# The up product of an sLSTM feed-forward as three half-precision products, features split by GpSimd, convolution sums in a row

## The reference, cut to what matters

```python
xn = ln(x);  xc = silu(causal_conv(xn, 4 taps))
wx = [gi(xc), gf(xc), gz(xn), go(xn)]            # 64x64 matrices per head
raw = wx_t + h @ rk + b                          # per token, in order
lfm = m + log_sigmoid(fr);  mn = max(ir, lfm)
cn = exp(lfm-mn)*c + exp(ir-mn)*tanh(zr);  nn = exp(lfm-mn)*n + exp(ir-mn)
h  = sigmoid(og) * cn / nn
x  = x + groupnorm(h)
x  = x + (gelu(g) * v) @ wd,  [g, v] = ln(x) @ wu     # 256 -> 2 x 336 -> 256
```

## Time and profile before

| | us |
|---|---|
| median of 3 runs | 4049.7 (4048.94 to 4052.33) |
| profiled execution | 4048.4 |
| its span, first to last instruction | 4046.7 |

### The profile page before, as it was taken

How to read it: one execution, slowest core, us unless ns; L and a number is a source line. 1 busy time by engine, 2 the same in 40 slices (tenths; PEclk the granted TensorE clock), 3 DMA queues, 4 the chain that set the end, 5 groups by cost and what they waited for, 6 DMA issues and landing times. The chain is left out here.

```text
span 4046.7 us, 170045 instructions
## 1 busy us (share of the span) xinstructions
PE 3876.7 (96%) x70778; PEld 2189.0 (54%) x70778; DVE 3681.0 (91%) x10771; ACT 3256.1 (80%) x6720; POOL 2211.6 (55%) x2425
## 2 busy tenths in 40 slices
PE   6999999999999999999999998799999999999997
PEld 3555555555555555555555554466666666666664
DVE  7999999999999999999999998788888888888886
ACT  4999999999999999999999998466666666666665
POOL 3666666666666666666666666444344443444443
PEclk9999999999999999999999999899999999999998
DMA  2000111000000000000000000000000001000000
GB/s 77 21 23 23 48 54 51 21 23 23 21 23 23 21 23 23 21 23 23 21 23 23 21 23 24 17 22 23 31 24 23 23 22 33 23 22 22 26 21 9
DMA packets 101034, 105.27 MB, mean 26 GB/s; under 512 B 17536, under 2 KB 96032, under 8 KB 99768
## 3 DMA queue, kind: packets, MB, share of 16 engines
q1 hardware_dynamic: 100264, 94.39, 8.0%
HBM read 48.68 MB, written 17.69 MB: 16 GB/s over the span
## 5 line engine op out<-in xcount | busy, mean ns | idle before, releaser
L596 POOL TENSOR_TENSOR conv_products<-normed_features,conv_taps_by_token 128x256 f32<-128x256 f32 (+1 forms) x852 | 780.4, 916 | 609.7 <-DVE convolved_features L549 358.5
L309 PE MATMUL banks<-up_centred,after_cell_features 128*32 128x336 f32 x9088 | 759.6, 452 | 0.0
L786 POOL TENSOR_TENSOR exps_of_both_halves<-scores 128x256 f32<-128x256 f32 x512 | 419.1, 842 | 619.9 <-ACT scores L1042 614.7
L285 PE MATMUL banks<-down,hidden_features 112*32 112x256 f32 x6816 | 427.5, 384 | 0.0
L365 ACT ACT_TABLE_LOAD x284 | 364.4, 1283 | 52.7 <-PE banks L265 47.8
L586 POOL TENSOR_TENSOR conv_partial_sums<-conv_products,conv_partial_sums 128x512 f32<-128x512 f32 x284 | 364.8, 1285 | 66.6 <-DVEq L485 44.4
L1042 ACT ACTIVATE scores<-scores 128x512 f32<-128x512 f32 x512 | 305.4, 626 | 116.3 <-DVE scores L1190 115.4
L309 PEld LDWEIGHTS banks<-up_centred,after_cell_features 128*32 128x32 f32 x9088 | 237.2, 109 | 270.6 <-issue 270.6
L386 ACT ACT_TABLE_LOAD x284 | 364.4, 1283 | 5.0
L1190 DVE SCALAR_TENSOR_TENSOR scores<-banks,score_top 128x512 f32<-128x512 f32 x512 | 327.7, 681 | 27.0 <-PE banks L872 26.4
L258 PE MATMUL banks<-recurrent_weights,h_features 64*32 64x256 f32 x9088 | 311.7, 383 | 1.4 <-ACT h_features L358 1.4
(11 more groups left out here) (215 smaller groups left out, 10055.6 us busy)
## 6 DMA issues: line engine op xcount, KB each, us to landing
layer_inputs<-layer_outputs SPq DMA_DIRECT2D x284, 96.0 KB, 2.0
layer_inputs<-in_x SPq DMA_DIRECT2D x285, 32.0 KB, 1.8
x_scratch<-layer_outputs SPq DMA_DIRECT2D x284, 32.0 KB, 1.8
x_tokens<-in_x SPq DMA_DIRECT2D x32, 256.0 KB, 3.1
context_features<-in_ctx SPq DMA_DIRECT2D x32, 256.0 KB, 3.8
layers_out<-x_scratch SPq DMA_DIRECT2D x32, 256.0 KB, 2.9
out<-result SPq DMA_DIRECT2D x64, 128.0 KB, 1.8
up_centred<-in_ff_up SPq DMA_DIRECT2D x1, 2688.0 KB
```

The lines of the kernel that those rows point to most:

```text
L285: mm = nc.tensor.matmul(bank[group(l), FD, 0:D], hidt[:, i, group(l)], down[:, l, i, :], start=i == 0, stop=i == UTILES - 1, skip_group_ch ...
L309: mm = nc.tensor.matmul(bank[group(l), b, 0:UP], xmt[:, n, group(l)], up[:, l, n, at:at + UP], start=n == 0, stop=n == HALF - 1, skip_grou ...
L596: nc.gpsimd.tensor_tensor(prod[:, i:i + n], xnt[:, j % NRING].rearrange("p n t -> p (n t)")[:, None, :].broadcast_to([P, n, HALF * P]), ta ...
L786: nc.gpsimd.tensor_tensor(psum[:, i % RING, :], pr[:, i % RING, 0:S], pr[:, i % RING, S:2 * S], ALU.add).then_inc(halves_added, 1)
```

## The change

**Up product.** Its weights `up` are scaled by 16 and split, ahead of the first step, into two half-precision parts `up_hi` (ACT) and `up_lo` (DVE). In each step the features `xmt` are split by POOL into `xmt_hi` (a cast) and `xmt_lo` (a subtraction). The product is then hi x hi + lo x hi + hi x lo; the factor 1/16 goes into `rs2`, which POOL makes from the reciprocal standard deviation. PE waits for `xmt_hi` ahead of the up product and for `xmt_lo` ahead of its last part.

**POOL.** The sums of 256 columns no longer wait for DVE; they follow `rs2` in a row. The products no longer wait for DVE either; the first waits for the copy of xn, and the others follow the split.

**Around them.** `centred` multiplies both heads at once by a block with zeros (8 matmuls of 128 columns, not 16 of 64). h is one instruction of 256 columns on DVE and is transposed by four plain matmuls. DVE makes `yn` and `xm` earlier. ACT copies xn's features ahead of Gelu, and the hidden features at the start of the next step. `up`, `rows` and `rows_rest` lie in memory that the second stage fills later.

```diff
+            def feed_up_gate(j):
+                pe.wait_ge(xmt_hi_done, j + 1)
+                for part in range(2):
+                    for n in range(HALF):
+                        feed_up(UPG, 0, n, part, first=part == 0 and n == 0)
+                for part in range(2):
+                    feed_up(UPV, UP, 0, part, first=part == 0)
+                pe.wait_ge(xmt_split, j + 1)
+                for n in range(HALF):
+                    feed_up(UPG, 0, n, 2, last=n == HALF - 1)
+                feed_up(UPV, UP, 0, 2)
...
-            def feed_up(b, at, n):
+            def feed_up(b, at, n, part, first=False, last=False):
+                w_, x_ = ((up_hi, xmt_hi), (up_lo, xmt_hi), (up_hi, xmt_lo))[part]
...
-                        for odd in range(2):
-                            r = slice(DH * odd, DH * odd + DH)
-                            at = UP + n * DH
-                            mm = nc.tensor.matmul(bank[group(l), UPG + odd, at:at + DH], ht[r, n, group(l)], gnc[r, l, n, :],
-                                                  start=n == 0, stop=True, skip_group_check=True)
+                        mm = nc.tensor.matmul(bank[group(l), UPG + n, UP:UP + P], ht[:, n, group(l)],
+                                              gnc[:, l, n].rearrange("p r d -> p (r d)"), start=True, stop=True, skip_group_check=True)
...
-                transposes(FD, D, h, ht_ready)
+                for n in range(HALF):
+                    for odd in range(2):
+                        i = odd * HALF + n
+                        mm = nc.tensor.matmul(bank[DH * odd:DH * odd + DH, FD, D + n * P:D + (n + 1) * P], h[:, i * DH:(i + 1) * DH], ident[:],
+                                              start=True, stop=True, skip_group_check=True)
...
-                for n in range(HALF):
-                    nc.vector.scalar_tensor_tensor(out=h[:, n * P:(n + 1) * P].rearrange("p (r d) -> p r d", r=2), in0=heads_of(ot[:], n),
-                                                   scalar=1.0, in1=heads_of(half_r[:], n), op0=ALU.add,
-                                                   op1=ALU.mult).then_inc(h_done, 1)
+                nc.vector.scalar_tensor_tensor(out=h[:], in0=ot[:], scalar=1.0, in1=half_r[:], op0=ALU.add,
+                                               op1=ALU.mult).then_inc(h_done, 1)
...
-                pool.wait_ge(xn_done, j + 1)
+                pool.wait_ge(rstd_step, 2 * j + 2)
+                nc.gpsimd.tensor_scalar(rs2[:], rs[:, HEADS:HEADS + 1], 1.0 / UP_SCALE, None, ALU.mult).then_inc(rs2_done, 1)
                 nc.gpsimd.tensor_tensor(new[:, 2], prod[:, 2], old[:, 3], ALU.add).then_inc(conv_shifted, 1)
-                pool.wait_ge(d_ready, j + 1)
                 nc.gpsimd.tensor_tensor(new[:, 3], prod[:, 3], old[:, 4], ALU.add).then_inc(conv_shifted, 1)
-                pool.wait_ge(xnt_copied, j + 1)
                 pool.wait_ge(conv_done, j + 1)
                 pool.wait_ge(conv_shifted, 2 * j + 2)
-                for i, n, after, count in ((0, 1, xm_done, j + 1), (1, 1, cell_step, 3 * j + 1), (2, 2, xs_done, j + 1)):
-                    pool.wait_ge(after, count)
+                pool.wait_ge(xnt_copied, j + 1)
...
+                conv_taps(0, 1)
+                pool.wait_ge(xmt_copied, j + 1)
+                if j > 0:
+                    pool.wait_ge(up_done, j)
+                nc.gpsimd.tensor_copy(xmt_hi[:], xmt[:]).then_inc(xmt_hi_done, 1)
+                pool.wait_ge(xmt_hi_done, j + 1)
+                nc.gpsimd.tensor_tensor(xmt_lo[:], xmt[:], xmt_hi[:], ALU.subtract).then_inc(xmt_split, 1)
+                conv_taps(1, 1)
+                conv_taps(2, 2)
```

More of the change, by code:

```diff
@@ L120, in slstm @@
     BIAS = 2 * 512
-    rows = sb("bias_rows", [3 * LAYERS, BIAS])
-    rows_rest = sb("bias_rows_rest", [3 * LAYERS, BIAS])
+    lent = kept["sums"][:].rearrange("p a n -> p (a n)")
+    rows, rows_rest = lent[0:3 * LAYERS, 0:BIAS], lent[0:3 * LAYERS, BIAS:2 * BIAS]
+    pieces = kept["pieces"]
     rows_hi, rows_mid, rows_lo = (sb("bias_hi", [3 * LAYERS, BIAS], F16), sb("bias_mid", [3 * LAYERS, BIAS], F16),
@@ L305, in hidden_features @@
                 mm.then_inc(hidt_ready, 1)
-            def feed_up(b, at, n):
+            def feed_up(b, at, n, part, first=False, last=False):
+                w_, x_ = ((up_hi, xmt_hi), (up_lo, xmt_hi), (up_hi, xmt_lo))[part]
                 for l in range(LAYERS):
-                    mm = nc.tensor.matmul(bank[group(l), b, 0:UP], xmt[:, n, group(l)], up[:, l, n, at:at + UP], start=n == 0,
-                                          stop=n == HALF - 1, skip_group_check=True)
-                return mm
+                    mm = nc.tensor.matmul(bank[group(l), b, 0:UP], x_[:, n, group(l)], w_[:, l, n, at:at + UP], start=first, stop=last,
+                                          skip_group_check=True)
+                return mm
+            def feed_up_gate(j):
[9 more added lines that the diff above has]
+                feed_up(UPV, UP, 0, 2)
             def feed_up_last():
-                feed_up(UPV, UP, 1).then_inc(up_done, 1)
+                for part in range(3):
+                    mm = feed_up(UPV, UP, 1, part, last=part == 2)
+                mm.then_inc(up_done, 1)
             pe.wait_ge(w_step, UP_SCALED)
@@ L361, in both @@
                 return ap.rearrange("p n t -> p (n t)")
+            for l in range(LAYERS):
+                for m in range(HALF):
+                    act.wait_ge(up_centred, HALF * l + m + 1)
+                    nc.scalar.activation(up_hi[:, l, m, :], up[:, l, m, :], ACT.Copy, scale=UP_SCALE).then_inc(up_hi_done, 1)
             act.wait_ge(first_gates, 1)
@@ L374, in _ @@
                 nc.scalar.activation(bank[:, FD, D:], spb[:], ACT.Ln, bias=1.0).then_inc(sp_step, 1)
+                if j > 0:
+                    act.wait_ge(hidt_ready, j)
+                    copy(both(hidt[:]), bank[0:UT, CV, 0:UTILES * P], hidt_copied)
                 act.wait_ge(gn_mv, HEADS * (j + 1))
@@ L388, in _ @@
                     act.wait_ge(up_done, j)
-                act.wait_ge(yn_done, j + 1)
-                nc.scalar.activation(gl[:], bank[:, UPG, 0:UP], ACT.Gelu, scale=rs[:, HEADS:HEADS + 1]).then_inc(gelu_done, 1)
                 act.wait_ge(xnt_ready, j + 1)
                 copy(both(xnt[:, j % NRING]), bank[:, CV, 0:D], xnt_copied)
+                act.wait_ge(yn_done, j + 1)
+                act.wait_ge(rs2_done, j + 1)
+                nc.scalar.activation(gl[:], bank[:, UPG, 0:UP], ACT.Gelu, scale=rs2[:]).then_inc(gelu_done, 1)
                 act.wait_ge(decay_step, 2 * j + 2)
@@ L401, in _ @@
                 nc.scalar.activation(ct[:], part[:, j % 2, 0], ACT.Tanh).then_inc(ct_done, 1)
-                act.wait_ge(hidt_ready, j + 1)
-                copy(both(hidt[:]), bank[0:UT, CV, 0:UTILES * P], hidt_copied)
-            act.wait_ge(hidt_copied, STEPS)
+            act.wait_ge(hidt_ready, STEPS)
         @block.vector
@@ L412, in _ @@
                 nc.vector.memset(buf[:], val).then_inc(w_step, 1)
+                n += 1
+            for odd in range(2):
+                nc.vector.memset(gnc[DH * odd:DH * odd + DH, :, :, 1 - odd], 0.0).then_inc(w_step, 1)
                 n += 1
@@ L476, in _ @@
                     w_ = up[:, l, m, :].rearrange("p (k n) -> p k n", k=2)
[L477 to L478 removed]
+                    nc.vector.tensor_tensor(w_, w_, bank[:, 2 * l:2 * l + 2, 0:UP], ALU.subtract).then_inc(up_centred, 1)
+            for l in range(LAYERS):
+                for m in range(HALF):
+                    dve.wait_ge(up_hi_done, HALF * l + m + 1)
+                    nc.vector.scalar_tensor_tensor(out=up_lo[:, l, m, :], in0=up[:, l, m, :], scalar=UP_SCALE, in1=up_hi[:, l, m, :],
+                                                   op0=ALU.mult, op1=ALU.subtract).then_inc(up_split, 1)
+            dve.wait_ge(up_split, LAYERS * HALF)
             dve.wait_ge(w_step, n)
```

63 lines of the change are left out of this document (36 added, 27 removed).

## The result

The changed kernel takes 4418.4 us (median of 4 runs, 4408.1 to 4421.7), the kernel before beside it 4049.3 (4 runs). The ratio is 1.0906, with a 95% interval of 1.0886 to 1.0926: 369 us slower. The forecast was 4435, range 4090 to 4500. The profiled run took 4408.1 us.

A forecast was written before the change was run, and what follows sets the result against it. VectorE (DVE) was taken to set the step, with TensorE (PE) close behind. The profiled 4048 us plus 381 (284 steps x 1.34 us) plus 7 for set-up gave about 4435 us, range 4090 to 4500.

The forecast's parts named there:

- The turn: A DVE instruction reading two SBUF tensors waits until the POOL instruction under way is done, then needs 0.28 us.
- the timetable: One step laid out from Gelu's start, placing POOL's split and products against DVE; 1.34 us more a step, chance 0.45.
- The two dearest terms: DVE stalls behind POOL's products: convolved features behind the 512-column product, 1.10 us; h behind tap 1, 0.45 us.
- the hinge: h asks 0.15 us behind tap 1; slightly more POOL work ahead would give the milder turn, 4180 us, chance 0.30.
- the stall of after_cell: After-cell (xm) on DVE waits for POOL's second sum: 0.30 us a step.
- The step without stalls: DVE's step less the waits of lines 532 and 526 and h's second instruction: 8.16 us.
- The sum: Profiled 4048.4 us, plus 284 steps of 1.34 us, plus 7 us set-up: about 4435 us.
- DVE sets the step, with PE close behind.: In the kernel before, DVE's timeline has hardly a hole, so it bounds the step of 8.67 us.
- The up product: On PE, half-precision groups replace fp32 ones: four groups save 0.56 us a step.
- Nothing together: On PE, the new centring matmuls and the four plain matmuls for h were taken to add or save nothing.
- The split: POOL's added work: cast 0.39 us, subtraction 0.66 us, one-column multiply 0.15 us a step.
- Rival 2: Stalls do not come and the engines' savings do: 8.3 us a step, about 3950 us; chance 0.20.

The follow-up runs named there:

- Experiments 1 and 2: 1: changed kernel, POOL's long product made to wait for the convolved features, 4096.0 us. 2: kernel before, POOL's waits for DVE taken out, 4486.5 us.
- Experiment 3: Changed kernel with two idle one-column multiplies added on POOL between the subtraction and tap 1: 4103.4 us.
- experiment 4: Two edits of the kernel before: POOL products moved off line 532, 4047.6 us; h as one DVE instruction with four plain matmuls, 4107.9 us.
- e12: Changed kernel with the split on ACT and DVE, POOL's gates as before, and the low part behind the cell's second DVE instruction: 3989.1 us, ratio 0.9851.
- e7: Changed kernel with the fp32 up product, no split, and POOL's list and waits of before; other edits kept: 4091.5 us, ratio 1.0106.
- experiment 6: Four kernels, each on the one before: changed kernel with split off POOL, 4056.2 us; POOL's gates back, 4044.7; h in halves, 4064.1; instead low part later, 3989.1.
- e2: Changed kernel with both of POOL's last products, tap 1 and the long one, waiting for the convolved features: 4079.7 us, ratio 1.0069.
- e11: Kernel before with h as one DVE instruction, transposed by four plain matmuls instead of two transposes: 4107.9 us, ratio 1.0145.

## Why the prediction was right

**The turn.** Right in kind and in size. Counted from the start of Gelu, at 1003.10 in the step shown, the timetable came true: hi starts at 1.45 (forecast 1.47), h ends at 3.58 (3.57), the convolved features end at 4.99 (5.01). The two dearest terms were 1.10 for the convolved features and 0.45 for h; the rows give 1.07 and 0.49. Experiments 1 and 2 show the cause both ways: one wait put back takes 322 us away, and the waits taken out of the old kernel add 436. Experiment 3 shows the hinge.

**The term that was mis-sized** is the stall of after_cell, "0.30 us": it is 0.12 in the mean, and minus_decay_logit has 0.07 where I had "none". After_cell and the second sum (line 628) start within 0.03 us of each other. In 151 of 192 steps after_cell got in first, and then it was POOL that waited: line 628 takes 1.03, not 0.73. In the other 41 the sum got in first, and after_cell waited for 0.56. The timetable allowed one order only. In all the stalls are 1.75 us and not 1.85, which is most of the 0.11 by which the step came out shorter than forecast (1.23 more than before, not 1.34).

**The step without stalls**, forecast at 8.16 us: after_cell's starts give (2399.1 - 507.1) / 191 = 9.906 us a step over the stretch of the groups, and less 1.75 that is 8.16.

**The sum** was built on a profiled run: 387 us more than its 4048.4. The profiled run after is 360 more; the medians are 369 apart. The changed kernel's four runs lie 14 us apart and its profiled one is the shortest of them, which nothing here explains, so the median lies nearer to the forecast than the rows do.

**What failed: "DVE sets the step, with PE close behind."** In the kernel before, the step hangs on PE's work and on the part of DVE's list that PE waits for (experiment 4). DVE's timeline without holes was read as a bound, but line 532 held a wait of 0.36, which is slack inside a row. On this point the forecast survived by luck: it rested on DVE's own sum, and with 1.75 us of stalls DVE does set the step. As a rule for a gain it would have misled: it prices 532's stall at 100 us, and it is worth nothing.

**PE.** The up product saved what was forecast, 0.56 us. These are PE's rows in e12:

```profile
1000.32 0.47 PE L316 MATMUL banks<-up_centred_hi,after_cell_features_hi 128*32 128x336 f16 x8
...
1001.72 0.54 PE L310 MATMUL banks<-identity,hidden 128*112 128x128 f32 x3
...
1002.77 0.33 PE L316 MATMUL banks<-up_centred_hi,after_cell_features_hi 128*32 128x336 f16 x4
...
1003.33 1.10 PE L267 MATMUL banks<-recurrent_weights,h_features 64*32 64x256 f32 x32
```

Three groups take 1.40 us (1.84 before), and the last one 0.56 (0.70), 0.58 less together. That the size was right is luck: 1.90 us in the earlier trace rows are three groups and not four, so four fp32 groups take 2.54 and not the 2.3 of the forecast, and the half-precision ones take 1.96 and not 1.7. The two misses cancel. "Nothing together" for the centring and h was wrong by 0.29 us against the change (e7). PE's busy share is 86%, not 80%.

**The split.** Cast 0.40 for 0.39 and subtraction 0.68 for 0.66. The multiply is 0.21, not 0.15. The set-up cost 7.0 us, as forecast.

**Rival 2**, the gain, was possible, but not with the split on POOL: experiment 6 got 59 us of its 100 by taking that work off POOL, keeping POOL's gates and moving one DVE instruction.

## What to carry to other kernels

A wait in POOL's list that reads nothing may be what keeps POOL out of VectorE's way; before you take it out, lay the two timelines side by side and ask which instruction will be under way when the other asks. A long row without idle time ahead of it may be a wait, and an engine whose rows hold waits need not be the bound, however full its timeline looks. When a stall is taken away and little comes back, look where the freed engine now waits, and move the work that waits there one instruction later.

## What the runs showed of the hardware that was not expected

- Turns are not only for two tensor inputs: a DVE tensor_scalar with one fp32 input and its output in SBUF took 0.82 us, not 0.41, and ended 0.15 us behind POOL's sum (e2, line 544). Not every instruction on SBUF does so: in the changed kernel the statistics of after_cell took 0.41 us from 1008.01, while POOL's sum ran from 1007.88.
- An instruction with one input in PSUM ran free: in e12 the low part (from PSUM and SBUF) took 0.42 us from 1008.72 while POOL's two products ran:

```profile
1008.07 1.48 POOL L637 TENSOR_TENSOR conv_products<-normed_features,conv_taps_by_token 128x256 f32<-128x256 f32 x2
```

- POOL waits too, if DVE asks first: the same 256-column sum took 0.73, or 1.03 with after_cell ahead of it.
- POOL's cast to half precision took 0.40 us in the changed kernel and 0.61 in e2. Which DVE instruction stood in its way there was not tried.
- Four plain fp32 matmuls that transpose 64 columns each take 0.59 us to the next start, and two transposes of 128 columns 0.37.
- The same recurrence matmuls take 0.89 us to the next start ahead of centring matmuls of 64 columns, and 1.02 ahead of those of 128 (before and e11 against e7).
